# Attention and experts of a graph block: gate by two token tiles, stack transfers on K's high part, upper-head units one slot further on

## The reference

```python
def _L0_gnn_ref(x, adj, Wq, Wk, Wv, Wg, bg):
    ...
    scores = jnp.einsum('bqhd,bkhd->bhqk', q, k) / jnp.sqrt(jnp.float32(DK))
    mask = (adj != 0)[:, None, :, :]
    scores = jnp.where(mask, scores, -jnp.inf)
    attn = jax.nn.softmax(scores, axis=-1)
    c = jnp.einsum('bhqk,bkhd->bqhd', attn, v).reshape(b, n, h)
    gate = jax.nn.sigmoid(jnp.concatenate([c, x], axis=2) @ Wg.T + bg)
    return gate * x + (1.0 - gate) * c
...
x = x + _L0_gnn_ref(_layernorm(x, axis=-1), adj, ...)
x = x + _L0_ffn_ref(_layernorm(x, axis=-1), L0_ffn_router_w, ...)
```

## Time and profile before

| what | before |
|---|---|
| median of 3 runs (lowest, highest) | 1842.68 us (1841.36, 1845.65) |
| the profiled execution, its own time | 1845.24 us |
| its span, first to last instruction | 1843.5 us |
| PE busy | 1739.2 us, 94% |
| DVE busy | 1272.6 us, 69% |
| ACT busy | 1101.4 us, 60% |
| POOL busy | 654.2 us, 35% |
| first and last S(p) start | 26.4 and 885.6 us |

### The profile page before, as it was taken

The page is one execution under the profiler, slowest core; times in us unless marked ns, Lnnn a source line. Parts: engine busy times, 40 slices in busy tenths (PEclk is TensorE's granted clock), DMA queues, the critical chain, the costliest instruction groups (busy, mean ns, idle before and its releaser), DMA issues. The chain is left out here.

```text
span 1843.5 us, 36156 instructions
## 1 busy us (share of the span) xinstructions
PE 1739.2 (94%) x12613; PEld 1459.3 (79%) x12613; DVE 1272.6 (69%) x3153; ACT 1101.4 (60%) x2509; POOL 654.2 (35%) x479
## 2 busy tenths in 40 slices
PE   5999999899999999999799999999999999999996
PEld 4677777677777777777587888788888988898986
DVE  5667777777776777777554564577778777877773
ACT  4888888888888888888533333233444443434442
POOL 0135444345544444553230100014433343344334
PEclk8999999999999999999899999999999999999998
DMA  5444565555455555555232354346546556555553
GB/s 148 132 141 130 159 171 169 151 155 149 146 166 161 164 164 156 148 147 166 81 104 92 115 172 149 127 161 166 167 139 171 137 163 167 161 165 162 135 151 38
DMA packets 140947, 269.21 MB, mean 146 GB/s; under 512 B 15072, under 2 KB 92256, under 8 KB 135776
## 3 DMA queue, kind: packets, MB, share of 16 engines
q1 hardware_dynamic: 113760, 230.45, 40.6%
q0 software_dynamic: 26592, 35.67, 9.5%
q10 hardware_dynamic: 416, 0.79, 0.2%
HBM read 141.99 MB, written 74.52 MB: 117 GB/s over the span
## 5 line engine op out<-in xcount | busy, mean ns | idle before, releaser
L836 DVE CUSTOM_DVE_ANT_0 pf<-bank,bias_q 128x512 f32<-128x512 f32 x512 | 348.0, 687 | 207.2 <-PE bank L480 194.3
L1188 POOL DMA_INDIRECT out_x<-yb,ix x142 | 245.1, 1726 | 570.8 <-ACT yb L1412 465.9
L609 ACT ACTIVATE pf<-pf,nmax 128x512 f32<-128x512 f32 x512 | 373.4, 729 | 50.5 <-DVE nmax L836 45.4
L1424 ACT ACTIVATE ah<-am 128x512 fp32r<-128x512 f32 (+1 forms) x220 | 133.1, 605 | 441.2 <-DVE am L1492 439.7
L1323 PE MATMUL bank<-xh,wh 128*128 128x512 f32 (+1 forms) x880 | 337.0, 383 | 0.9 <-ACT pt L597 0.9
L490 PE MATMUL bank<-ident,pf 128*128 128x128 f32 x2048 | 312.6, 275 | 26.0 <-ACT pt L597 25.3
L1324 PE MATMUL bank<-xl,wh 128*128 128x512 f32 (+1 forms) x880 | 336.3, 382 | 0.0
L1325 PE MATMUL bank<-xh,wl 128*128 128x512 f32 (+1 forms) x880 | 336.2, 382 | 0.0
L490 PEld LDWEIGHTS bank<-ident,pf 128*128 128x128 f32 x2048 | 252.5, 141 | 82.6 <-issue 35.8
L597 ACT ACTIVATE pt<-bank 128x512 f32<-128x512 f32 x512 | 307.2, 600 | 12.9 <-PE bank L490 12.8
L480 PE MATMUL bank<-stack 96*128 96x512 f32 x512 | 237.1, 463 | 31.4 <-DMA stack<-qk 16.6
(11 more groups left out here) (209 smaller groups left out, 3147.6 us busy)
## 6 DMA issues: line engine op xcount, KB each, us to landing
raw<-in_w_all SPq DMA_DIRECT2D x39, 1536.0 KB, 6.8
stack<-qk SPq DMA_DIRECT2D x378, 128.0 KB, 2.4
xb<-xg_dram SPq DMA_DIRECT2D x32, 520.0 KB
adj_i<-in_adj SPq DMA_DIRECT2D x32, 512.0 KB, 5.1
xn<-in_x SPq DMA_DIRECT2D x16, 512.0 KB, 6.4
xn_dram<-xn SPq DMA_DIRECT2D x16, 512.0 KB
xp<-in_x SPq DMA_DIRECT2D x16, 512.0 KB, 6.7
xnp<-xn_dram SPq DMA_DIRECT2D x16, 512.0 KB, 7.9
```

Of the source, the lines that this page charges most:

```text
L609: act.activation(pf[i][:, :], pf[i][:, :], ACT.Exp, bias=nmax[:, i:i + 1], scale=-1.0, accum_out=den[:, g, tq, j:j + 1]).then_inc(p_exp, 1)
L836: dve.tensor_tensor_reduce(pf[r][:, :], S[p % 2][:, :], bias_q[1 - par][:, tq, :], -SCALE, -3.0 * MASKED, ALU.add, ALU.min, nmax[:, r:r + ...
L1188: pool.indirect_dma_start(out=out, out_offset=bass.IndirectOffsetOnAxis(ap=ix[n % RING][:, i:i + 1], axis=0), in_=yb[s][:, i, :], in_offse ...
```

## The change

- L0, M0, Q1, K1, V0 and V1 stand one slot later; C0 to X1 stay. `choose`, `mark` and ACT's `exp` of the routing follow by one slot, `bias0` goes from slot 4 to 6, `weigh` from 6 to 13, `stat` from 8 to 12 (where `var` is).
- `gate` and `x1` work on two token tiles at a time: the first half in slots 17 and 18 (after Z1), the second in 19 and 20 (after Z3). `stat2` goes from slots 21 and 22 to 19 and 21. `s_mix` counts four for each batch and no longer two.
- For the lower heads SP now waits for Q0's low part and K0's high part, sends two of the three transfers of all four heads, then waits for K0's low part and sends the four that hold it.
- R0's fourteen matmuls of 8 columns become five of 32, 24, 16, 8 and 32 columns.

```diff
-UNIT_AT = {"L0": 0, "M0": 1, "Q1": 2, "K1": 4, "V0": 6, "V1": 8, "C0": 10, "C1": 11, "R0": 12, "Z0": 14, "Z1": 15, "Z2": 16,
+UNIT_AT = {"L0": 1, "M0": 2, "Q1": 3, "K1": 5, "V0": 7, "V1": 9, "C0": 10, "C1": 11, "R0": 12, "Z0": 14, "Z1": 15, "Z2": 16,
...
-            for rows, (a, c) in enumerate([(QH, KH), (QL, KH), (QH, KL)]):
+            for rows in part:
+                a, c = [(QH, KH), (QL, KH), (QH, KL)][rows]
...
-                    refs(B, unit(b, "K0") + 1, range(0, GRP, 2) if first(b) else range(GRP))
+                    if first(b):
+                        refs(B, unit(b, "K0") + 1, range(0, GRP, 2))
+                    else:
+                        sp.wait_ge(g_free, unit(b, "Q0") + 1)
+                        sp.wait_ge(g_hi, hi_index(b, "K0") + 1)
+                        sp.nop().then_inc(s_held_sp, 1)
+                        for r in range(GRP):
+                            send_head(sp, r, range(2))
+                        sp.wait_ge(g_free, unit(b, "K0") + 1)
+                        for r in range(GRP):
+                            send_head(sp, r, range(2, 3))
...
-                    for i in range(NT):
-                        pe.matmul(o[:, E * i:E * i + E], below[:, :], mb[:, i, :], start=True, stop=False)
-                        for j in range(i):
-                            pe.matmul(o[:, E * i:E * i + E], ones_b[:, :], mb[:, j, :], start=False, stop=False)
-                        last = pe.matmul(o[:, E * i:E * i + E], ones_b[:, :], msum[:, :], start=False, stop=True)
+                    oe = o[:, 0:NT * E].rearrange("p (i e) -> p i e", e=E)
+                    pe.matmul(oe, below[:, :], mb[:, :, :], start=True, stop=False)
+                    for j in range(NT - 1):
+                        pe.matmul(oe[:, j + 1:NT, :], ones_b[:, :],
+                                  mb[:, j:j + 1, :].to_broadcast([P, NT - 1 - j, E]), start=False, stop=False)
+                    last = pe.matmul(oe, ones_b[:, :], msum[:, :].rearrange("p (o e) -> p o e", o=1)
+                                     .to_broadcast([P, NT, E]), start=False, stop=True)
...
+                for half in range(2):
+                    hs = slice(half * NT * D // 2, (half + 1) * NT * D // 2)
+                    if post and p == DVE_AT["gate"][half]:
...
+                        dve.wait_ge(g_free, unit(b, "Z3" if half else "Z1") + 1)
+                        dve.wait_ge(s_d, A * 2 + 2)
+                        dve.scalar_tensor_tensor(out=df[:, hs], in0=zf[:, hs], scalar=1.0, in1=df[:, hs],
+                                                 op0=ALU.add, op1=ALU.mult).then_inc(s_mix, 1)
```

36 lines of the change are left out of this document (15 added, 21 removed).

## The result

The changed kernel takes **1823.8 us** (median of 5 runs, 1822.27 to 1833.15), against 1842.68 before on the same chip (five runs by now, 1840.27 to 1845.65). The ratio is 0.9905, 95% interval 0.9877 to 0.9933: about 1% faster. The forecast was 1817 with a range of 1808 to 1831. So the time lies in the range, but the gain is 19 us where 26 were expected. The profiled execution of the changed kernel took 1823.8 us, with a span of 1822.1; that of before took 1845.24 and 1843.5.

What follows compares the result with a forecast made beforehand. PE sets the attention stage's pace, losing time in four places a batch. 16.1 + 4.2 - 0.8 + 3.5 + 5.5 - 2.6 = 25.9 us off 1845.24 gives 1819.3, median about 1817; range 1808 to 1831.

Steps and rivals of the forecast that it cites:

- the queue: SP's sends before S(0): rivals had issues rarely standing still, 1809 us, or mostly standing still, 1832; chance 0.12 each.
- Part 1: Slots 8 to 12: moving `stat` to slot 12 ends waits of PE and lateness of ACT, gaining 16.1 us.
- small things: Side effects such as bias0, the mask's later second half and POOL's later `xn`: all put at nothing.
- Part 2: Units one slot on: X1's copy `z` no longer delays slot 0, gain 4.2 us; V1's later copy costs 0.8.
- Part 5: Stack transfers: S(0) waits 0.9 to 1.0 us a batch, against some 12 us of old waits; net -2.6 us.
- Part 3: Slot 12: R0 with five matmuls for fourteen saves 0.25 us a batch, 3.5 us in all.
- Part 4: Slots 17 to 25: halved gate and x1 and earlier stat2 remove ACT's 0.39 us wait in slot 25; gain 5.5 us.
- The fixed cost of two more instructions: Halved gate and x1 on DVE: 0.32 us a batch, taken as nothing; by the skill's rule alone, 1822 us.
- a shorter landing: Stack transfers: with the skill's fixed cost of about 2.0 us, S(0) comes 0.3 us sooner, 1812 us.
- The experts' half: The part of the kernel outside the attention stage: untouched, no change forecast.
- the waits come back: Slots 12 to 14: late DVE or ACT loses half or all of the `stat` gain, 1825 to 1833 us; chance 0.16.

Runs made afterwards that it cites:

- e10: Changed kernel with the four statistics instructions back in slot 8 and the units of the upper heads in their old slots: 1832.1 us, ratio 0.9958.
- e6: Changed kernel with only the four statistics instructions put back in slot 8 from slot 12: 1813.0 us, ratio 0.9845.
- e7: Changed kernel with the units of the upper heads (L0, M0, Q1, K1, V0, V1) back in their old slots: 1827.1 us, ratio 0.9906.
- e5: Changed kernel with POOL's eight row scatters taken out of slots 19 and 20: 1820.1 us, ratio 0.9886.
- e1: Changed kernel with the twelve stack sends as before, head by head, all behind K0's low part: 1842.8 us, ratio 1.0016.
- e3: Changed kernel with R0 as the fourteen small matmuls of the kernel before: 1833.0 us, ratio 0.9953.
- e4: Changed kernel with gate, x1 and second statistics in their old slots, gate and x1 still cut in halves: 1845.6 us, ratio 1.0019.
- e11: Changed kernel with the statistics back in slot 8, and gate, x1 and second statistics in their old slots: 1821.0 us, ratio 0.9899.
- e12: Changed kernel with the statistics back in slot 8 and the twelve sends as in the kernel before: 1829.8 us, ratio 0.9944.

## Why the prediction was right, and where it was not

The range held the time, and the sign was right. But 1823.8 us lies outside the 1812 to 1822 of the forecast itself, and the sum lacked a term of about 11 us that it had put at nothing. That the range held is owed to its width, made for other reasons (the queue, and waits that did not come back), and in that it was luck. A batch takes 52.90 us and not the 52.2 forecast. Point by point, per batch:

- **Part 1, stat at 12 (16.1 us).** The step that failed. Its size was read well: 1.15 us were forecast and the crowding costs 1.17 (e10 against e6 and e7). That size is paid once, though: the units' move alone frees nearly as much, so that undoing the move to slot 12 alone changes slots 8 to 13 by nothing (e6). Since the prediction claimed it once, this is no error of its sum. The error is what the move costs elsewhere. What it does do stood in the prediction among the small things, at no cost: "POOL norms `xn` 1.2 us later, six slots before P0." P0 was the wrong consumer to look at. Behind `xn` on POOL stand the eight scatters; they lost their slack, and ran back to back over slots 19 and 20. This costs slots 20 to 24 0.72 us, which e5 shows too, and slots 25 to 27 0.24 (3.54 against 3.30), which only e6 shows; 11 us in the medians of e6 and the changed kernel. In the other order, with the units in their old slots, it is the same: from e10 to e7 slots 8 to 13 win 1.17 us and slots 20 to 27 lose 0.94, so of the 16.1 us about 3 are left.
- **Part 2, units (4.2 - 0.8 us).** The 0.09 us for V1's copy are there (e7). The 0.3 us for `z` were a true loss of the kernel before, whose slot 0 takes 1.83 us with the wait. But in e7 and e10 slot 0 takes 1.44 us without it, although L0 stands in slot 0 again: S(0)'s own wait for the sends goes ahead of it there. So this gain is not the units' once part 5 is made, and the 0.32 us of e7 agree with the 0.3 by luck. With the old sends the units' move costs slots 31 to 3 0.60 us (e1: 6.82 + 0.71 against 6.93). Besides, this part carries the whole 16 us of part 1 once the statistics are back in slot 8 (e10).
- **Part 3, R0 (3.5 us).** 0.21 to 0.22 us a batch against 0.25 (e3).
- **Part 4, gate (5.5 us).** The idle of ScalarE in slot 25 is 0.39 us in e4 and 0 in the changed kernel, as the rows of before had it; slots 25 to 27 confirm 0.42 (e11). The fixed cost of two more instructions, which the Trainium skill (VectorE: DVE Perf Modes, the section on the TRN2 errata) speaks for, shows in no slot: those of the first halves, 17 and 18, take 2.21 and 1.03 us before and after, so it was hidden. Not seen was that this part matters three times as much when slot 20 starts late (1.24 us in e4 against 0.40 in e11).
- **Part 5, sends (-2.6 us).** The wait before S(0) was well forecast: 1.09 us on average (slot 31: 1.78 against 0.69) against 0.95, and 0.46 in quiet batches against 0.4. Against the kernel before, with the units in their old slots, the forecast of 0.17 us of loss holds too: slots 31 to 3 take 7.04 (e10) or 7.25 us (e7, one batch at half clock) against 6.93. The sign was wrong for the part as it stands in this change. I set the new wait against the 12 us of send waits of the kernel before. But with part 2 made, slots 0 to 3 have 0.71 us less work and no wait for `z`, and late heads would wait that much more: S(3) can't be earlier than head 3 lands. The comparison that counts is with the old sends in the new order, and there the early sends gain 19 us (e1) or 17 (e12). Parts 2 and 5 together come out right again, at 0 (6.93 against 6.22 + 0.71) where 0.1 was forecast. The sends of the changed kernel between 700 and 712 us took 2.4 us to land (median), so a shorter landing, by which the prediction had reckoned 1812 us as well, did not come.
- **Small things.** Batch 0 was to change by little ("spare DVE time"); it took 3.1 us more. The four bn_stats of its slots start at 46.57 us, not at 42.12, POOL's `xn` is 1.65 us later, and since these slots are short, P0 waits for it:

```profile
55.36 0.72 PE L411 MATMUL bank<-ident,xn 128*128 128x128 f32 x4 [1.47 <-POOL xn L957]
```

  This lengthens slot 18 by 0.9 us. Behind it the clock is at half, which it was not in this batch before:

```profile
55.76:59.17 3.41, 3.41 (x17) 2.96 (x14) 1.44 (x5) 3.25 (x8) 0.00 (x0) 0.50 0.46 159
```

  Slots 19 and 20 take 1.2 us more. Another 1.1 us is S(0)'s wait. That e6 did not get slot 18 back has a second cause, which the prediction had put at nothing: the mask's second half. SP issues its load behind the twelve sends of heads 4 to 7, at 49.59 before and 50.51 us after, and DVE's wait for it grows from 1.76 to 2.67 us. In e6 the load is issued at 51.84, and with `xn` early it is the mask for which S(19) waits; DVE's row, then PE's:

```profile
55.57 0.69 DVE L685 TENSOR_SCALAR bias_q<-adj_i 128x1024 bf16<-128x1024 int32 x1 [2.77 <-DMA adj_i<-in_adj]
...
57.02 0.59 PE L493 MATMUL bank<-stack 96*128 96x512 f32 x1 [1.50 <-DVE nmax L849]
```

  There too the clock is at half behind the wait, from 57.22 to 60.63 us. In the changed kernel the two waits cover each other: DVE is done with S(17)'s tile, the first that needs the mask, only at 55.57, and S(19) starts at 55.74, so P0's wait costs hardly more than the mask's would alone.
- **The experts' half.** No change was forecast, and the 6.6 us between the two profiles are within what this half scatters by (950.4 to 959.3 us), the clock being lower in the profile of before (0.984 against 0.988).

The sum with what the runs showed, per batch: 1.30 (crowding, by before and e7; 1.17 by e10) + 0.21 (R0) - 0.09 (V1's copy) + 0 (slots 31 to 3, units and sends together) + 0.61 (slots 25 to 27, 3.91 against 3.30) + 0.05 (slots 4 to 7 and 14 to 19) - 0.96 (POOL) = 1.12, against 1.14 measured. The forecast had 1.15 + 0.25 + 0.3 - 0.05 + 0.39 - 0.17 = 1.87. The difference is POOL's term, less the 0.22 more of slots 25 to 27.

The rival "the waits come back" gave a time near the measured one, 1825 to 1833, by a mechanism that isn't there: no wait of PE for `ct_l`, and 0.09 us for V1's copy.

## What to carry to other kernels

When a change has several parts, cost each against the kernel with all the others made, and not against the kernel before: two moves that relieve the same crowded slots pay once, whether they take work from the late engine or give the waiting one something to do meanwhile, and a part that looks like a loss may be what lets another pay. When a step is moved, follow what it releases through the whole queue of the engine that waits for it, to the last instruction that shares it, and not only to the first consumer; an engine that is idle 65% of the time can still be the one that must not be late. And a wait that the trace shows is worth only what the other engines don't use it for: of 1.1 us before S(0), 0.56 could be had, and with the statistics in slot 8 about 0.1. Before a difference in a few slots is put down to an edit, look at the granted clock there: one stretch at half clock in thirteen batches made 0.12 us of a mean.
